# An LSTM record encoder on one core: order of lookup, sums, tanh and index digits changed, and the last layer's weights moved

## What is computed

```python
def lstm_last(x, Wx, Wh, b):            # gates i, f, g, o
    def step(carry, xt):
        h, c = carry
        i, f, gg, o = jnp.split(xt @ Wx + h @ Wh + b, 4, axis=-1)
        c = sigmoid(f) * c + sigmoid(i) * tanh(gg)
        h = sigmoid(o) * tanh(c)
        return (h, c), None
...
m_from = lstm_last(base_emb[from_seq], seq_Wx, seq_Wh, seq_b)      # 64 steps, H = 64
m_to   = lstm_last(base_emb[to_seq], seq_Wx, seq_Wh, seq_b)
# 11 features, 32 steps, H = 8; x = [num_emb[numbers], freq_emb[freqs]], tables of 1000 rows
nwf = vmap(enc)(...)
feats = concat([goby, bool, bool, m_from, m_to, count, count, nwf])
return relu(feats @ reduce_W + reduce_b)
```

## Time and profile before

| | before |
|---|---|
| median of 3 runs | 1712.03 us (1711.87 to 1713.39) |
| profiled execution, its own time | 1714.94 us |
| its span, first to last instruction | 1713.1 us |
| busy: PE, DVE, ACT, POOL | 94%, 88%, 77%, 56% |
| mean granted PE clock | 0.989 of full speed |

### The profile page before, as it was taken

The page is one execution under the profiler, slowest core; times in us unless marked ns, Lnnn a source line. Parts: engine busy times, 40 slices in busy tenths (PEclk is TensorE's granted clock), DMA queues, the critical chain, the costliest instruction groups (busy, mean ns, idle before and its releaser), DMA issues.

```text
span 1713.1 us, 57020 instructions
## 1 busy us (share of the span) xinstructions
PE 1610.2 (94%) x23780; PEld 619.1 (36%) x23780; DVE 1509.0 (88%) x1573; ACT 1314.0 (77%) x2011; POOL 955.3 (56%) x473
## 2 busy tenths in 40 slices
PE   3799999999999999999999999999999999999997
PEld 0233333333333333333333333333333333333334
DVE  6788988989988989988989988988988988988984
ACT  4577777877777877777877778877778877778874
POOL 1445666776666776666754444554444554444553
PEclk8899999999999999999999999999999999999999
DMA  8678789898889898889788789899889888788870
GB/s 285 223 253 261 248 263 276 264 276 271 256 268 284 250 284 260 270 264 284 251 287 262 260 263 277 260 275 267 273 265 280 256 277 274 256 267 273 248 241 24
DMA packets 165793, 444.19 MB, mean 259 GB/s; under 512 B 45728, under 2 KB 103584, under 8 KB 132640
## 3 DMA queue, kind: packets, MB, share of 16 engines
q1 hardware_dynamic: 162112, 439.63, 81.8%
q0 software_dynamic: 2560, 0.15, 0.6%
q10 hardware_dynamic: 864, 0.75, 0.1%
HBM read 423.42 MB, written 6.82 MB: 251 GB/s over the span
## 4 chain that ended last, share of the span: by engine, by line
PE 53%; DVE 17%; ACT 15%; issue 9%; POOL 2%; DVEq 0%; POOLq 0%; ACTq 0%
PE e_ps L479 16%; PE ab L619 11%; PE f_ps L619 9%; PE ab L511 7%; DVE kept L493 7%; ACT gate L673 5%; DVE f_ps L705 5%; DVE seq_c L710 4%; ACT f_ps L671 3%; PE ab L425 3%; ACT tanh_c L664 3%; PE ab L560 2%; POOL ig L697 2%; ACT f_ps L673 2%; PE ab L570 2%
## 5 line engine op out<-in xcount | busy, mean ns | idle before, releaser
L697 POOL TENSOR_TENSOR ig<-gate 128x1024 f32<-128x1024 f32 x192 | 411.9, 2145 | 696.3 <-ACT seq_x L432 293.7
L479 PE MATMUL e_ps<-hot,tab 128*32 128x512 bf16 x8448 | 527.5, 384 | 61.6 <-DVE kept L493 56.8
L493 DVE SCALAR_TENSOR_TENSOR kept<-high,cst,e_ps 128x1024 f32<-128x1024 uint8 x352 | 449.1, 1276 | 49.6 <-PE e_ps L479 43.8
L619 PE MATMUL ab<-seq_h,seq_wh 64*64 64x512 f32 x3024 | 401.2, 590 | 0.0
L479 PEld LDWEIGHTS e_ps<-hot,tab 128*32 128x32 bf16 x8448 | 214.0, 97 | 486.8 <-issue 342.7
L469 DVE TENSOR_SCALAR hot<-low,cst 128x4096 bf16<-128x4096 bf16 x256 | 320.6, 1281 | 13.2 <-PE e_ps L479 13.2
L731 POOL TENSOR_TENSOR seq_h<-gate,tanh_c 128x1024 f32<-128x1024 f32 x128 | 308.9, 2414 | 31.8 <-ACT tanh_c L664 31.6
L673 ACT ACTIVATE gate<-ab,nwf_bias 128x512 f32<-128x512 f32 (+2 forms) x384 | 188.4, 553 | 166.2 <-PE ab L570 103.0
L671 ACT ACTIVATE gate<-ab 128x1024 f32<-128x1024 f32 x256 | 262.5, 1026 | 17.6 <-PE ab L619 8.8
L664 ACT ACTIVATE tanh_c<-seq_c 64x512 f32<-64x512 f32 (+1 forms) x384 | 241.9, 630 | 29.8 <-POOL nwf_h L731 22.1
L664 ACT ACTIVATE gate<-ab 64x512 f32<-64x512 f32 (+1 forms) x384 | 228.5, 595 | 9.4
(11 more groups left out here) (99 smaller groups left out, 1809.1 us busy)
## 6 DMA issues: line engine op xcount, KB each, us to landing
low<-low_digits SPq DMA_DIRECT2D x256, 1024.0 KB
low<-low_bytes SPq DMA_DIRECT2D x96, 512.0 KB
tok<-seq_tokens SPq DMA_DIRECT2D x128, 384.0 KB
high<-high_digits SPq DMA_DIRECT2D x1408, 32.0 KB
nwf_hq<-nwf_h SPq DMA_DIRECT2D x62, 128.0 KB
raw<-in_indices SPq DMA_DIRECT2D x32, 176.0 KB
low_digits<-low_of SPq DMA_DIRECT2D x32, 88.0 KB, 3.2
nwf_hq<-nwf_h SPq DMA_DIRECT2D x62, 32.0 KB, 3.0
```

Of the source, the lines that this page charges most:

```text
L479: last = nc.tensor.matmul(e_ps[32 * g:32 * g + 32, i, :], tab[:, part, 2 * m + ty, :], hot[:, p % HOT_RING, g, i, :], start=(part == 0), s ...
L493: nc.vector.scalar_tensor_tensor(out=kept[:, p % KEPT_RING, :, :], in0=wanted, scalar=cst[:, C_HIGH:C_HIGH + 1], in1=e_ps[:, :, :], op0=AL ...
L619: last = nc.tensor.matmul(flat(bank)[to:to + 64, cols], lhs(rows, half, block), rhs(rows, block, a, b), start=start, stop=stop)
L697: nc.gpsimd.tensor_tensor(ig[:, cols], gates[0][:, n % 2, cols], gates[1][:, n % 2, cols], ALU.mult).then_inc(ig_ready, 1)
```

## The change

Five things are done.

1. In the small cell PE does the lookup before the sums. In S cells PE does gate 1 before the sums; ACT follows, and `USES` with them.
2. ACT takes `tanh_of(n-1)` in S cells behind gate 1 and the copy of the sums (before: behind gate 0), and in the large cell ahead of gate 0 (before: behind gate 1). In the small cell it stays behind gate 1. In the last cell it comes behind the copy of the sums, not ahead of it.
3. The digits of rounds 3 to 31 are made three cells earlier, in the small cell two rounds ahead instead of the large cell, and behind the cell's one compare. SP's stores and the next load of raw indices move with them from S0 to S2.
4. The dense weights have SBUF tensors of their own. They are loaded ahead of the cells, without a wait for `low`.
5. `place_dense_w` is done in cell 16 (the large cell of round 2) instead of the last cell.

```diff
-ROUND_AT = {(0, 3)[_r - 1] if _r < 3 else NUMBER["nwf", _r - 2, 0]: _r for _r in range(FIRST_ROUNDS, NWF_T)}
+ROUND_AT = {(0, 3)[_r - 1] if _r < 3 else NUMBER["nwf", _r - 3, 1]: _r for _r in range(FIRST_ROUNDS, NWF_T)}
...
-        USES += [("gate", _n, 0), *_x, ("gate", _n, 1)]
+        USES += [("gate", _n, 0), ("gate", _n, 1), *_x]
...
-        dense_row = end[:, rows_at:dense_at].rearrange("p (f o) -> p f o", f=FEATURES)
-        dense_w = end[:, dense_at:dense_at + 4 * FEATURES * OUT].rearrange("p (f s o) -> p f s o", f=FEATURES, s=4)
+        dense_row = sb("dense_row", [P, FEATURES, OUT], F32)
+        dense_w = sb("dense_w", [P, FEATURES, 4, OUT], F32)
...
# SP
+                sp.dma_start(dense_row[:, :, :].rearrange("p f o -> p (f o)"), dense_rows).then_inc(dense_here, 16)
                 for n in range(NCELLS):
...
-                    if n == LAST_SEQ + 1:
-                        sp.wait_ge(hot_ready, ALL_PAIRS)
-                        sp.dma_start(end[:, rows_at:dense_at], dense_rows).then_inc(dense_here, 16)
...
# DVE
+                    elif n == 16:
+                        place_dense_w(dve)
                     for p in compared[:2]:
                         compare_pair(dve, p)
-                        if p == compared[0] and n in ROUND_AT and CELLS[n][0] == "nwf":
-                            make_digits(dve, ROUND_AT[n])
+                    if n in ROUND_AT and CELLS[n][0] == "nwf":
+                        make_digits(dve, ROUND_AT[n])
                     for p in pairs[1:]:
                         keep_wanted(dve, p)
                     for p in compared[2:]:
                         compare_pair(dve, p)
-                    if n == LAST:
-                        place_dense_w(dve)
                     scale_c(dve, n)
...
# ACT
+                    if CELLS[n][0] == "seq":
+                        activate(act, n, 0)
+                        activate(act, n, 1)
                         store_sums(act, n)
                         if n:
                             tanh_of(act, n - 1)
+                        if later_seq(n) is not None:
+                            seq_store_x(act, later_seq(n))
+                        activate_f(act, n)
+                    else:
+                        store_sums(act, n)
+                        if CELLS[n][2] == 0 or n == LAST:
+                            tanh_of(act, n - 1)
+                        activate(act, n, 0)
+                        activate(act, n, 1)
+                        if CELLS[n][2] and n < LAST:
+                            tanh_of(act, n - 1)
+                        activate_f(act, n)
                     activate(act, n, 3)
...
# PE
                         gate(pe, n, 0)
                         for p in pairs[:1]:
                             look_up(pe, p)
+                        gate(pe, n, 1)
                         sums(pe, n)
-                    else:
+                    elif large:
                         sums(pe, n)
                         for p in pairs[:1]:
                             look_up(pe, p)
+                    else:
+                        for p in pairs[:1]:
+                            look_up(pe, p)
+                        sums(pe, n)
                         if not large:
                             gate(pe, n, 0)
+                            gate(pe, n, 1)
                     if large:
                         gates_of_large(pe, n, 0, 1)
-                    else:
-                        gate(pe, n, 1)
```

More of the change, by code:

```diff
@@ L235, in build @@
         rows_at = y_at + SLOTS * OUT
-        dense_at = rows_at + FEATURES * OUT
         small = end[:, 0:y_at]
         y = end[:, y_at:rows_at].rearrange("b (s o) -> b s o", s=SLOTS)
-        dense_row = end[:, rows_at:dense_at].rearrange("p (f o) -> p f o", f=FEATURES)
-        dense_w = end[:, dense_at:dense_at + 4 * FEATURES * OUT].rearrange("p (f s o) -> p f s o", f=FEATURES, s=4)
+        dense_row = sb("dense_row", [P, FEATURES, OUT], F32)
+        dense_w = sb("dense_w", [P, FEATURES, 4, OUT], F32)
         ab = [ctx.enter_context(nc.psum_tensor(f"ab{n}", [P, 2, CH], F32)) for n in range(2)]
@@ L761, in place_dense_w @@
             dve.wait_ge(dense_here, 16)
-            nc.vector.tensor_tensor(dense_w, dense_row[:, :, None, :].to_broadcast([P, FEATURES, 4, OUT]),
+            nc.vector.tensor_tensor(dense_w[:, :, :, :], dense_row[:, :, None, :].to_broadcast([P, FEATURES, 4, OUT]),
                                     cst[:, None, C_SLOT:C_SLOT + 4, None].to_broadcast([P, FEATURES, 4, OUT]),
@@ L940, in _ @@
                 for n in range(NCELLS):
[L941 to L944, removed]
+                    if CELLS[n][0] == "seq":
+                        activate(act, n, 0)
+                        activate(act, n, 1)
                         store_sums(act, n)
-                    activate(act, n, 0)
-                    if is_seq:
                         if n:
                             tanh_of(act, n - 1)
+                        if later_seq(n) is not None:
+                            seq_store_x(act, later_seq(n))
+                        activate_f(act, n)
+                    else:
                         store_sums(act, n)
[L951 to L956, removed]
+                        if CELLS[n][2] == 0 or n == LAST:
[5 more added lines that the diff above has]
+                        activate_f(act, n)
                     activate(act, n, 3)
```

## The result

The changed kernel takes **1781.76 us** (median of 4 runs, 1779.5 to 1783.91) against 1712.71 for the kernel before on the same chip: a ratio of 1.0399 [1.0379, 1.042], 69 us slower. Forecast were 1751 and a range of 1686 to 1758. Sign, place and the collision came as written; what it costs did not. (One slip ahead of the prediction: the work is cut into 192 cells, not 193. No number hangs on it.

What follows compares the result with a forecast made beforehand. PE, busy 94% of the span and mostly waiting for DVE's `e_ps`, was taken as the bound. Net +1.30 a round over 29 rounds, +37.7, plus +1.3 for the rest, on 1712.03 gave 1751 us; range 1686 to 1758.

Steps and rivals of the forecast that it cites:

- The collision in the small cell: Small cell: POOL's `ig` and `new_h` get in between linked digit instructions and hold DVE; second lookup of S2 2.21 us later.
- The seam: From large cell to S0: without the digits there, the second lookup starts at 920.88 against 921.79, a gain of 0.91 us.
- behind that lookup everything shifts together: After the second lookup of S2: S2, S3 and large cell, bound by PE, shift by the delay; net +1.30 us a round.
- more collisions: Rival: DVE, 2 us late in S2, meets POOL again, or SP's stores are late; over 1758 us, chance 0.06.
- the tail: End of the kernel: f 0.3 us earlier and the copy ahead of tanh, 0.3; -0.6 us in all.
- Rounds repeat closely: Steady part: 14 rounds from the large cell at 909.52 to that at 1628.51 take 51.36 us each, the last 50.50.
- Tanh in S cells: Tanh behind gate 1 in S cells: taken at 0; without its cover each 0.1 late costs 3 us in all.
- The dense weights in round 2: Large cell of round 2: placing takes 3.08 us, the seam loses its 0.91 and 1.0 more; +1.9 us, once.
- The load at the start: Dense weights' load moved to the start, ahead of pair 4: 0 to 1.8 us, taken at 0.5.
- The digits slip through: Rival: `new_h` asks after the sixth digit instruction starts, the last two run unbroken; -0.87 us a round, 1688 us, chance 0.18.
- the 0.3 us: Small cell: margin between tanh of S1 and the digits, said to decide whether `new_h` gets in before the sixth instruction.
- POOL doesn't get in between: Rival: DVE holds on through its linked digit instructions; about -0.54 us a round, 1697 us; chance 0.08 together with no collision.

Runs made afterwards that it cites:

- POOL's wait: Changed kernel, but in small cells with digits POOL waits until DVE has made them before `ig`: 1708.93 us, 0.9976 of the kernel before.
- tanh behind f: Changed kernel, but in small cells with digits ACT does the forget gate before tanh of the cell before: 1696.45 us, 0.9901 of the kernel before.
- PE's hole filled: Changed kernel with the short sum of S2 computed four times into the same place, 48 more matmuls a round: 1754.24 us, 1.025 of the kernel before.
- sheltered digits: Changed kernel with POOL waiting for the digits in small cells; with tanh also put back at its old places in S cells and large cell, 1721.89 us.
- the digits moved back: Changed kernel with the digits put back into the large cell, between its two compares, all else as changed: 1707.27 us, 0.9968 of the kernel before.
- the kernel with digits alone: Kernel before with only the digits moved, to the small cell behind its compare: 1802.54 us, 1.0523 of the kernel before.

## Why the prediction was wrong in size and right in kind

*The collision in the small cell* held step by step. Forecast were 1.1 us for the second digit instruction and 2.5 for the sixth; they take 1.00 and 2.40 in nearly all rounds. Forecast was a loss of 2.21 at the second lookup of S2; measured are 1.92 (lookup to lookup 7.80 + 5.23 + 4.24 for 6.08 + 3.38 + 5.89), so the term was 0.3 too large. Three kernels take the collision away, each in another way: POOL's wait and the digits ahead of the compare keep the engines apart, tanh behind f keeps `new_h` off the digits. They win back 73, 75 and 85 us.

*The seam* was forecast at 0.91, measured 0.89 (5.02 + 3.94 for 6.08 + 3.77). A clean round nets +1.02, forecast +1.30.

**The step that failed** is the line under the collision, "the second lookup of S2 starts at 947.56 instead of 945.35. Loss 2.21 us", with "behind that lookup everything shifts together". It priced PE's idle time at its own length. After it, in 18 of the 29 rounds with digits, PE runs 3.4 us at half clock, and the round loses 1.64 more: 29.5 us in all, more than the 26.6 us by which the forecast of the span (+39.0 for +65.6) fell short. The kernel with PE's hole filled shows it: 31.7 us back by the spans, 27.5 by the medians. In the profile of before the mean granted clock was 0.989, and I took that as constant. That trace had the sign in it: in rounds 0 and 1 PE is idle 2.56 and 3.04 us before a lookup, and a stretch of 3.4 us at 0.50 follows each. No rival held it; "more collisions" had the right side of the range for another reason.

*A second step failed* by the choice of a sample. The round at 909.52 was read as all rounds. It lies behind the gathers. In rounds 3 to 14 the large cell's gates take 0.7 longer, hidden under the very digits that were moved away: +8.4. The two items make 37.9, 11 more than the shortfall. Of these, 9.5 came back in terms that were priced too high: 0.28 for each of 29 rounds in the net of collision and seam, and 1.4 in the tail. "Rounds repeat closely" was true of their length and not of what bounds them.

*The rest.* Tanh in S cells was taken at 0; what it does beside the collision was not measured alone. Beside sheltered digits the new places of tanh are worth 0.65 a round, 0.27 of it at the seam and the rest in S cells. The order of lookup and sums, for which the sum has no term, gave 0.25 to 0.3 a round in S2 with the digits moved back. The dense weights in round 2 cost 3.0 where 1.9 were forecast, the tail gained 2.0 where 0.6 were, a part of it by the clock (3.4 us at 0.50 for 6.8). The load at the start shows no cost: rounds 0 and 1 together moved by 0.5 besides their clock falls.

*The rivals.* The digits slip through: it did not come about, but tanh behind f confirms its mechanism and nearly its price (50.35 a round for 50.49). How exactly the 0.3 us decide was not tried: that edit moves `new_h` by much more. POOL doesn't get in between: refuted. By the rows `new_h` even starts (1087.96) while L359 runs (1087.91 to 1088.16); L360, which waits for L359, is then the one held. The rule of the Trainium skill (SBUF — State Buffer, "Who interferes with whom") that an instruction holds the shared ports for its whole length agrees with all these rows: 1.00 for 0.25 beside `ig`, 2.40 for 0.34 beside `new_h`.

## What to carry to other kernels

An idle time of PE is not priced at its length: look, in the stretch behind existing gaps of about that length, at the granted clock, and add the slower matmuls if it falls, in some of the rounds or in all. Before work is moved out of a place, ask what it hid there, in rounds of every kind and not in one sample, and before short DVE instructions are moved to another place, lay POOL's instructions over them: a wait on POOL, or one ACT instruction in another order, was worth 73 and 85 us here. The worth of a small part of a change is to be measured once the large loss beside it is gone.

## What the runs showed of the hardware

- The granted clock fell to 0.50 for 3.4 us around PE's return from an idle time of 1.97 to 2.57 us, in 18 of the 29 rounds with digits. In the other 11 the same lookup came at nearly the same distances (7.80 and 5.1 to 5.3 after the two before it) and the clock stayed at 1.00. After 0.66 us idle (the filled kernel) it never fell. Length alone doesn't decide: with the digits moved back PE is idle 3.04 and 3.28 us in rounds 1 and 2, and no fall follows.
- What sorts the rounds was not tried by a run. The Trainium skill (TensorE: Matmul & The Clock Gate, "What's actually happening") says that the monitor looks at the array's activity in windows that run freely, not from the kernel's start. That would let equal gaps end differently. The trace agrees so far: from round 5 to 8 the falls start 54.61 us apart (394.25, 448.87, 503.48, 558.09) while the rounds between take 54.74 to 54.77, so that they come ever earlier against the lookup, 1.25 us behind its start and then 1.08, 0.95 and 0.81.
- A digit instruction that meets a POOL instruction is long by about what POOL's takes: 1.00 us for 0.25 beside `ig`, 2.40 for 0.34 beside `new_h`. Most of those that were hit had to wait for the one before (L336 and L360; L337 and L358 in the kernel with digits alone). That is no condition: L361, which waits for nothing of its own, took 2.5 us for 0.33 in cell 3 and in rounds 2 and 10.
- Small gathers issued by POOL lengthen the large cell's gates on PE from 2.42 to 3.1 us when they fall into S3 and the large cell. Kept to the other four cells they leave the gates at 2.42 in every round, and 14 of the 20 rounds with gathers take 50.34 or 50.35, as most of those without do. The path of this stays open.
